# Value matmuls of a latent attention in groups of 6 key tiles in place of 3, with a ring of 12 probability tiles

## The reference, cut to what matters

```python
q_big = _apply_rope(einsum('bshk,hkq->bshq', q_hk, w_kc_q), sin_q, cos_q)
kv_r = _apply_rope(kv_c, sin_k, cos_k)              # (8, 1444, 64)
q_r = einsum('bshq,hqr->bhsr', q_big, W_qr)
k_r = einsum('bld,hdr->bhlr', kv_r, W_kr)
attn = softmax(einsum('bhsr,bhlr->bhsl', q_r, k_r), axis=-1)
ctx_c = einsum('bhsl,bld->bhsd', attn, kv_r)        # the value matmuls
ctx = einsum('bhsd,hkd->bhsk', ctx_c, w_kc_kv) ...  @ Wo.T
```

## Time and profile before

| what | value |
|---|---|
| median of 3 runs | 1904.63 us (1898.18 to 1914.96) |
| the profiled execution | 1914.01 us, its span 1912.3 us |
| TensorE busy | 1666.3 us, 87% of the span, 7692 matmul instructions |
| VectorE, ScalarE, GpSimd busy | 999.3, 664.7, 802.3 us |
| mean granted TensorE clock | 0.915 of 2.4 GHz |
| the stage ST_XB | about 640 to 1213 us |

### The profile page before, as it was taken

How to read it: one execution, slowest core, us unless ns; L and a number is a source line. 1 busy time by engine, 2 the same in 40 slices (tenths; PEclk the granted TensorE clock), 3 DMA queues, 4 the chain that set the end, 5 groups by cost and what they waited for, 6 DMA issues and landing times. The chain is left out here.

```text
span 1912.3 us, 22038 instructions
## 1 busy us (share of the span) xinstructions
PE 1666.3 (87%) x7692; PEld 1208.8 (63%) x7692; DVE 999.3 (52%) x1459; ACT 664.7 (35%) x1062; POOL 802.3 (42%) x529
## 2 busy tenths in 40 slices
PE   6976999976999799899999899597979797689998
PEld 3756999973444465565566565345555555489998
DVE  2653444422466665665665663457363636334444
ACT  2333444421233233323323324154343434233333
POOL 2722434413344376766667757123232323023332
PEclk8897999985999799998899899798989898889999
DMA  1011222125000011011011000100000000144331
GB/s 36 1 34 52 75 75 75 58 68 149 20 20 1 32 47 48 1 47 47 1 47 47 17 1 1 68 1 23 22 22 22 22 22 0 33 114 124 118 118 59
DMA packets 71900, 84.53 MB, mean 44 GB/s; under 512 B 8108, under 2 KB 58220, under 8 KB 71830
## 3 DMA queue, kind: packets, MB, share of 16 engines
q1 hardware_dynamic: 71830, 83.62, 14.3%
HBM read 82.55 MB, written 0.95 MB: 44 GB/s over the span
## 5 line engine op out<-in xcount | busy, mean ns | idle before, releaser
L552 POOL TENSOR_TENSOR e_wl<-e_wf,e_wh 128x768 fp32r<-128x768 f32 x69 | 139.8, 2026 | 376.1 <-ACT e_wh L743 332.9
L638 POOL TENSOR_TENSOR xc<-xc,prob 121x800 f32<-121x800 f32 x112 | 226.1, 2019 | 117.8 <-ACT prob L852 111.5
L852 ACT ACTIVATE prob<-PS 121x800 f32<-121x800 f32 x192 | 158.5, 837 | 316.8 <-PE PS L1553 316.8
L1138 DVE TENSOR_REDUCE mx<-PS 128x1 f32<-128x482 f32 (+1 forms) x312 | 188.8, 651 | 133.8 <-PE PS L1533 131.7
L1411 PE MATMUL PS<-e_hh,e_wh 128*128 128x400 f32 x552 | 194.1, 352 | 14.6 <-DVE e_hl L1084 7.9
L1412 PE MATMUL PS<-e_hl,e_wh 128*128 128x400 f32 x552 | 192.0, 348 | 0.0
L1413 PE MATMUL PS<-e_hh,e_wl 128*128 128x400 f32 x552 | 191.2, 346 | 0.0
L1532 PE MATMUL PS<-kth,qs 128*128 128x482 f32 (+1 forms) x312 | 134.5, 431 | 37.9 <-DVE mx L1138 14.1
L758 ACT ACTIVATE e_sg<-PS 128x400 f32<-128x400 f32 x138 | 69.7, 505 | 272.1 <-PE PS L1413 272.1
L1568 PE MATMUL PS<-prob,kvn 121*64 121x400 f32 (+1 forms) x768 | 163.0, 566 | 0.0
L660 POOL TENSOR_TENSOR q<-q,qt 128x400 f32<-128x400 f32 x64 | 65.9, 1030 | 207.5 <-DVE qt L1247 207.5
(11 more groups left out here) (200 smaller groups left out, 3399.0 us busy)
## 6 DMA issues: line engine op xcount, KB each, us to landing
e_wb<-routing SPq DMA_DIRECT2D x32, 400.0 KB, 4.1
e_wf<-in_L_ffn_gate_up_proj SPq DMA_DIRECT2D x64, 128.0 KB, 2.3
krt<-in_ctx_T SPq DMA_DIRECT2D x8, 722.0 KB, 4.2
ksw<-in_ctx_Tswap SPq DMA_DIRECT2D x8, 722.0 KB, 6.2
e_wf<-in_L_ffn_down_proj SPq DMA_DIRECT2D x32, 128.0 KB, 2.2
wq<-in_L_ffn_Wq SPq DMA_DIRECT2D x4, 1024.0 KB, 5.0
wo<-in_L_ffn_Wo SPq DMA_DIRECT2D x4, 1024.0 KB, 5.2
e_wf<-in_L_ffn_Wg SPq DMA_DIRECT2D x32, 128.0 KB, 2.2
```

Of the source, the lines that this page charges most:

```text
L552: pool.tensor_tensor(m["wl"][:, slot], m["wf"][:, slot], m["wh"][:, slot].bitcast(fp32), ALU.subtract).then_inc(ms["wlo"], 1)
L638: pool.tensor_tensor(accp, accp, prob[:, n % RING], ALU.add).then_inc(xb["ap"], 1)
L852: act.activation(prob[0:k, n % RING], PS[0:k, 2 * (n % 2):2 * (n % 2) + 2, 0:GC], ACT.Exp).then_inc(xb["ex"], 1)
L1138: dve.tensor_reduce(mx3[:, m, g:g + 1], PS[:, 4 + k % 3, 0:SEG[g][1]], AX.X, ALU.max).then_inc(xb["free"], 1)
```

## The change

The ring of probability tiles grows from 6 to 12 (19.2 KB more a partition), and values() takes 6 key tiles a call. It is called at the steps with s % 6 == 2 from step 8 on, so the tiles 6c to 6c + 5 come at step 6c + 8. The thresholds of all waits on xb["pv"], which counts the calls, follow. Order and place of all else stay.

```diff
-    RING = 6
+    RING = 12
...
                     if b > 0:
-                        sp.wait_ge(xb["pv"], 8 * b)
+                        sp.wait_ge(xb["pv"], 4 * b)
                     load_values(b + 1)
...
-                    act.wait_ge(xb["pv"], m // 3 + 1)
+                    act.wait_ge(xb["pv"], m // 6 + 1)
...
             def keep_context(i):
 
-                act.wait_ge(xb["pv"], 4 * i + 4)
+                act.wait_ge(xb["pv"], 2 * i + 2)
...
             def values(c):
 
-                b, i = c // 8, c // 4
-                if c % 8 == 0:
+                b, i = c // 4, c // 2
+                if c % 4 == 0:
                     pe.wait_ge(xb["nrot"], 3 * (b + 1))
-                if c % 4 == 0 and i >= 1:
+                if c % 2 == 0 and i >= 1:
                     pe.wait_ge(xb["raw"], i)
-                pe.wait_ge(xb["ex"], 3 * c + 3)
-                for n in range(3 * c, 3 * c + 3):
+                pe.wait_ge(xb["ex"], 6 * c + 6)
+                for n in range(6 * c, 6 * c + 6):
...
-                    if s % 3 == 2 and 5 <= n < B * SP_ + 3:
-                        values((n - 5) // 3)
+                    if s % 6 == 2 and 8 <= n < B * SP_ + 3:
+                        values((n - 8) // 6)
```

## The result

The changed kernel takes 1941.64 us (median of 4 runs, 1931.57 to 1950.74) against 1906.16 us for the kernel before (4 runs by then): a ratio of 1.0184, 95% interval 1.0107 to 1.0261. It is slower by 35 us. The forecast was 1914, its range ended at 1931, so the result lies outside, 7.6 us past rival 2 (1934).

What follows compares the result with a forecast made beforehand. The stage was taken to go at TensorE's pace, less some 41 us standing still. Passages -8.4, handovers +11.8, small terms +0.3, +0.4, +1.5 and clock +4 gave +9.6 on the median 1904.63: 1914 us, range 1899 to 1931.

Steps and rivals of the forecast that it cites:

- rival 2: At each handover the clock falls once for the new hole and once for the old wait: +30 us, 1934; chance 0.13.
- The value groups: TensorE enters and leaves value matmuls 32 times for 63; 24 saved passages inside batches give 8.4 us.
- the waits of L1568 for issue: Sign that the forecast is right: these waits at the value matmuls would be halved.
- The price of a passage: TensorE's switch into and out of a value group: 0.09 entry, 0.15 inside, 0.11 exit, together 0.35 us.
- The handover: Between batches, step 0 starts at T+4.81 (T: start of the maxima's turn) after 2.0 us idling; +11.8 us in all.
- The small terms: Joined runs +0.3 us, the last group at the very end +0.4, VectorE's maxima +1.5.
- VectorE's +1.5: VectorE comes out late after step 3 in its maxima, 0.2 us a batch: +1.5 us (0 to 4).
- +5.6 us without the clock: Sum of the stage's terms before the clock: -8.4 + 11.8 + 0.3 + 0.4 + 1.5.
- The clock: New idling at seven handovers may each add a 3.41 us low stretch, 12 us at most; a third taken, +4.
- Rival 1: Not slower: longer value runs at steps 2 to 8 and 15 to 20 keep the clock up, 1898; chance 0.12.
- rival 3: VectorE becomes the bound in six-step runs without values, at worst +21 to the 5.6 us: 1931; chance 0.07.
- rival 4: The chain of the rows at the handover comes before T+2.79 and all is saving: -8.7 us, 1896; chance 0.05.

Runs made afterwards that it cites:

- keep23: The kernel before with a ring of 12 and the value groups of steps 5, 11 and 17 moved into 8, 14 and 20; 1.0071 of before.
- filled: The changed kernel with ten extra score matmuls, results thrown away, ahead of the wait for qm at the seven handovers; 1.0087 of before.
- early_values: The kernel before with three value groups moved ahead of key units: step 2's within its step, 5's and 17's to 4 and 16; 0.9766 of before.

## Why the prediction was wrong, point by point

- The value groups: right. 32 groups; one of 24 instructions takes 871.72 to 875.90, 4.18 us, against 2.16 + 2.01 by the prediction's rows. One sign did not come: the waits of L1568 for issue were not halved (73.3 us before, 78.7 after). The price of a passage was not measured by itself; keep23's stage is in keeping with it, the times of the runs are not.
- The handover: right to a tenth. Step 0 at T+4.80 for T+4.81, seven waits of 1.96 us in the mean for 2.0 (18.4 less 4.7 of the first batch). At the handover from batch 0 to 1, left open, the lateness went: from 728.24 to 733.03 are also 4.8 us, so it cost 0.2 and not 1.1.
- The small terms: VectorE's +1.5 was not there as such (mx 14.1 to 14.5 us). Against the +5.6 us without the clock the changed kernel leaves +1.4 at the rate of 0.42 and +11 at that of filled. The fairest measure is filled's profiled stage, with the clock of the kernel before: +7.8.
- The clock: this step failed, "I take a third of 12: +4". The runs showed 72 us more at 1.2 GHz, worth 20 to 30 us, and a clock of the stage of 0.87, below the 0.90 that was named as rival 2's sign. Two things were wrong in it. First, "one more stretch as short as" 3.41 us: at the handover shown the low stretch grew from 6.83 to 10.23 us and at all seven by 31 us in sum, and as much again came behind step 4 and around step 17, where the prediction had nothing. Second, the evidence against was misread. The prediction took it from the earlier trace rows that a hole of 1.49 us costs no clock, since from step 0 to the values 6.24 us pass there as elsewhere. The trace of the kernel before has the clock of that handover:

```profile
724.11:727.52 3.41, 2.07 (x10) 1.73 (x11) 1.60 (x3) 1.24 (x2) 3.41 (x2) 1.00 0.00 0
727.52:734.35 6.83, 5.79 (x18) 2.81 (x18) 4.36 (x4) 3.06 (x4) 4.52 (x3) 0.50 0.01 1
```

  The clock did fall, at 727.52, 2.3 us behind the hole and before the wait for L837 had begun, and sooner after step 0 than in the earlier trace rows (2.3 us for 4.2). The 6.24 us hid it, because what step 2 lost came out of that wait: it was 1.04 us long in place of 1.46. Between hole and fall TensorE had waited for nothing but 0.20 us for an activation.
- Rival 2 was the right mechanism, with 0.13 far too small a chance and 1934 still some us short; its one fall for each wait is not what the trace shows, but longer stretches and others elsewhere. The Trainium skill (TensorE: Matmul & The Clock Gate, the section on psum-queue depth-cycling) had said it: short idle times between groups of matmuls make the clock swing, and the throughput pays. Here the trace and filled agree, with 16 us won back by filling seven holes.
- Rival 1 was wrong in sign, rival 3 is not seen in the profile (VectorE's waits), rival 4 not in the DMAs.

## What to carry to other kernels

Before value work, or any filler, is moved to save a fixed cost, look at what it stands in front of: here several of the eight groups covered a chain of another engine, and the passages saved (11 us by the prediction's rows) were less than the one cover taken away. Price an idle hole on TensorE by what the clock does after it, which was here about twice the hole (20 to 30 us for 12.2), and look at the clock itself over every hole that is already there: equal times from step to step don't show that it stayed up. The cheap way up is the other way round: put work that is ready in front of what TensorE waits for (0.977 of before, with three calls moved).

## What the runs showed that was not expected

- Ten matmuls at each handover whose result is thrown away made the kernel 16 us faster (filled against the changed kernel), with step 0 no sooner after the turn.
- The clock was granted 1.00 over 430 us in early_values, in which no wait of TensorE was over 1.1 us; in all 14 profiles every fall to 1.2 GHz in this stage came in or within a few us of an idle time of 0.9 us or more (but not every such time brought one).
- A low clock can last with TensorE busy all the time: 900.55 to 910.79 above, without values, 3.41 us in the earlier trace rows with values behind. But 6.83 us (1099.57 to 1106.40) occur with them too, in the kernel before; what exactly brings the clock back is not settled.
- Runs of one kernel differ by up to 28 us (before, 1897 to 1925), and the clock goes with it: 0.927 in the fastest, 0.909 in the slowest.
